# A fused convolution, linear-attention and mixture-of-experts block on one core: two small products and the reciprocals' low halves move from VectorE to GpSimd, and the program orders of the engines are written anew

## What is computed

```python
x = x + conv3x3(sign(batchnorm(groupnorm(x))), sign(W) * scale)      # L0
t = x as 3136 tokens of 32 channels
u = layernorm(t)
q, k, v = elu(u Wq)+1, elu(u Wk)+1, u Wv                               # 16 heads of 32
o = (q cos) (k cos)^T v + (q sin) (k sin)^T v;   denom = 1 / (q . sum(k) + 1e-5)
t = t + (o * denom) Wd + bd                                            # L1, linear attention
p = softmax(layernorm(t) Wr + br); the two largest of 8, scaled to sum 1
t = t + sum over those two of p_e * (layernorm(t) We + be)             # L2, two experts of 8
```

## Time and profile before

| | us |
|---|---|
| median of 3 runs | 2692.53 (2686.22 to 2696.71) |
| profiled execution, span from its first to its last instruction | 2691.5 |
| busy: PE / DVE / POOL / ACT | 2363.6 / 2278.2 / 1865.1 / 1743.1 |
| share of the span | 88% / 85% / 69% / 65% |

### The profile page before, as it was taken

How to read it: one execution, slowest core, us unless ns; L and a number is a source line. 1 busy time by engine, 2 the same in 40 slices (tenths; PEclk the granted TensorE clock), 3 DMA queues, 4 the chain that set the end, 5 groups by cost and what they waited for, 6 DMA issues and landing times.

```text
span 2691.5 us, 57490 instructions
## 1 busy us (share of the span) xinstructions
PE 2363.6 (88%) x19300; PEld 1162.4 (43%) x19300; DVE 2278.2 (85%) x2849; ACT 1743.1 (65%) x2821; POOL 1865.1 (69%) x1479
## 2 busy tenths in 40 slices
PE   3479999999999999998999999899898999999972
PEld 3324444444444444444444444444444444444442
DVE  4457999898998989898898989999898989999973
ACT  0167777676776767666776767777676767777630
POOL 0124777777777777776777777777777777777677
PEclk7589999999999999999999999999999999999995
DMA  9200000000000000000000000000000000000000
GB/s 261 34 13 10 11 16 17 10 8 17 17 17 17 17 17 5 14 17 17 17 16 17 6 12 17 17 17 16 18 12 7 16 17 17 17 11 7 7 7 12
DMA packets 235817, 55.16 MB, mean 20 GB/s; under 512 B 229648, under 2 KB 230528, under 8 KB 235360
## 3 DMA queue, kind: packets, MB, share of 16 engines
q1 hardware_dynamic: 235488, 50.96, 9.4%
HBM read 31.19 MB, written 12.85 MB: 16 GB/s over the span
## 4 chain that ended last, share of the span: by engine, by line
PE 41%; DVE 32%; issue 17%; ACT 5%; POOL 2%; DMA 1%; DVEq 1%; SPq 1%; ACTq 0%; POOLq 0%
PE ps L606 7%; DVE kbuf L987 7%; PE ps L581 6%; DVE qbuf L993 5%; PE ps L572 4%; PE ps L623 4%; PE ps L597 3%; PE ps L564 3%; DVE route L1052 3%; PE ps L657 3%; PE ps L632 3%; DVE prod L1077 2%; DVE rs L1010 2%; ACT ebuf L717 2%; PE ps L645 2%
## 5 line engine op out<-in xcount | busy, mean ns | idle before, releaser
L712 ACT ACTIVATE ebuf<-ps,small 112x1024 f32<-112x1024 f32 x448 | 498.5, 1113 | 279.0 <-PE ps L572 242.0
L987 DVE SCALAR_TENSOR_TENSOR kbuf<-ps,ebuf 112x1024 f32<-112x1024 f32 x448 | 542.7, 1211 | 113.1 <-ACT ebuf L712 110.1
L811 POOL TENSOR_TENSOR qbuf<-spread_r,qbuf 128x896 f32<-128x896 f32 x224 | 473.9, 2116 | 179.4 <-ACT spread_r L747 179.3
L993 DVE SCALAR_TENSOR_TENSOR qbuf<-ps,ebuf 128x896 f32<-128x896 f32 x448 | 485.8, 1084 | 84.5 <-ACT ebuf L717 62.6
L717 ACT ACTIVATE ebuf<-ps,small 128x896 f32<-128x896 f32 x448 | 451.4, 1008 | 122.8 <-PE ps L597 71.1
L581 PE MATMUL ps<-kbuf,xcs 112*64 112x512 f32 x1792 | 488.8, 624 | 39.1 <-issue 32.7
L789 POOL TENSOR_TENSOR rstd<-varr,power 112x28 f32<-112x28 f32 x64 | 307.2, 4800 | 183.1 <-DVE varr L977 179.5
L632 PE MATMUL ps<-qbuf,gmat 128*64 128x224 f32 x3584 | 387.5, 358 | 39.4 <-DVE pbuf L1021 35.9
L840 POOL TENSOR_TENSOR prod<-prod 112x512 f32<-112x512 f32 x224 | 285.7, 1276 | 103.0 <-DVE prod L1077 103.0
L747 ACT ACTIVATE spread_r<-ps 128x896 f32<-128x896 f32 x224 | 205.5, 917 | 171.1 <-PE ps L623 162.0
L632 PEld LDWEIGHTS ps<-qbuf,gmat 128*64 128x64 f32 x3584 | 237.0, 137 | 157.0 <-DVE pbuf L1021 44.0
(11 more groups left out here) (133 smaller groups left out, 3530.2 us busy)
## 6 DMA issues: line engine op xcount, KB each, us to landing
qbuf<-in_x SPq DMA_DIRECT2D x8, 1568.0 KB, 11.6
xt<-in_x SPq DMA_DIRECT2D x256, 49.0 KB
out<-ffn SPq DMA_DIRECT2D x256, 49.0 KB
shifted<-nat SPq DMA_DIRECT2D x128, 52.6 KB, 5.0
qbuf<-in_sel SPq DMA_DIRECT2D x1, 1024.0 KB, 11.8
tabn<-in_tabnc SPq DMA_DIRECT2D x1, 784.0 KB, 13.5
p<-in_p2c SPq DMA_DIRECT2D x1, 528.0 KB, 10.4
tabd<-in_tabdc SPq DMA_DIRECT2D x1, 448.0 KB, 11.0
```

What stands on the lines that cost most here:

```text
L712: act.activation(ebuf[0:PT, 0, :].rearrange("p (a b) -> p a b", a=2), o[0:PT, :, :], ACT.Exp, bias=minus_one[0:PT, :]).then_inc(kexp_made, 1)
L811: nc.gpsimd.tensor_tensor(qbuf[:, 2:4, n, :], spread_r[:, :, :], qbuf[:, 2:4, n, :], ALU.mult)\
L987: v.scalar_tensor_tensor(kbuf[:, n % 2, :].rearrange("p (a b) -> p a b", a=2), o[0:PT, :, :], 1.0, ebuf[0:PT, 0, :].rearrange("p (a b) -> ...
L993: v.scalar_tensor_tensor(qbuf[:, k0:k0 + 2, j, :], o[:, :, 0:G * PT], 1.0, ebuf[:, 1, 0:2 * G * PT].rearrange("p (a b) -> p a b", a=2), AL ...
```

## The change

Four things are changed.

1. The remainder (RL) is made by POOL, one instruction for each half. It reads `den` and `r_high` in all 128 partitions, spread twice over the columns, and writes all of `rs`; ACT then overwrites one quadrant pair for each half of the columns with the high part (a new step RH, two copies that read `r_high`, behind a wait for POOL).
2. The two products of marks and rank (RF) are made by POOL. DVE's next reduction waits for each.
3. The first reduction and the first marking of the routing read the logits out of PSUM; DVE's copy is gone, and ACT makes it (LG on ACT), behind a wait for both DVE readers. The PSUM slot is given back by ACT's copy.
4. `schedule` and `SHIFTS` are replaced by one table of places for each engine (`ORDER`).

```diff
-SCHEDULE = schedule()
+ORDER = {
+    "tensor": {
+        "RP": [12.95, 13.20, 14.05, 15.50, 17.85, 18.99, 20.75],
...
+    "gpsimd": {
+        "RL": [13.11, 17.30],
+        "RF": [32.19, 33.81],
...
-                "LG": (route_step, 16), "F": (prod_made, 7), "XC": (xc_made[0], 1), "ZT": (z_made[0], 2), "ZU": (z_made[1], 2),
+                "LG": (logits_kept, 1), "F": (prod_made, 7), "XC": (xc_made[0], 1), "ZT": (z_made[0], 2), "ZU": (z_made[1], 2),
```

On ACT:

```diff
                 elif kind == "RC":
...
                     act.activation(r_high[:, :], den[:, 0:HALFW], ACT.Copy).then_inc(rhigh_made, 1)
+                elif kind == "RH":
+                    act.wait_ge(r_made, m.at(2, n + 1))
                     for c in range(2):
-                        last = act.activation(rs[0:64, n, HALFW * c:HALFW * (c + 1)], den[64 * c:64 * c + 64, 0:HALFW],
-                                              ACT.Copy)
+                        last = act.activation(rs[64 - 64 * c:128 - 64 * c, n, HALFW * c:HALFW * (c + 1)],
+                                              r_high[64 * c:64 * c + 64, :], ACT.Copy)
                     last.then_inc(r_rows_made, 1)
...
+                elif kind == "LG":
+                    act.wait_ge(route_step, m.at(13, 2))
+                    act.activation(route[:, 0, :], o[0:PT, 0, 0:SLOTS * EXPERTS], ACT.Copy).then_inc(logits_kept, 1)
```

On POOL:

```diff
+                elif kind == "RL":
+                    pool.wait_ge(rhigh_made, m.at(2, n + 1))
+                    both = [128, 2, HALFW]
+                    nc.gpsimd.tensor_tensor(rs[:, n, :].rearrange("p (c t) -> p c t", c=2),
+                                            den[:, 0:HALFW].unsqueeze(1).to_broadcast(both),
+                                            r_high[:, :].unsqueeze(1).to_broadcast(both), ALU.subtract).then_inc(r_made, 1)
+                elif kind == "RF":
+                    pool.wait_ge(route_step, m.at(13, 2 if n == 0 else 7))
+                    hot = route[:, 1 + n, :]
+                    nc.gpsimd.tensor_tensor(hot, hot, first[:, :], ALU.mult).then_inc(hot_ranked, 1)
```

On DVE:

```diff
-                elif kind == "RL":
-                    dve.wait_ge(rhigh_made, m.at(2, n + 1))
...
-                    last.then_inc(r_made, 1)
...
-                elif kind == "LG":
-                    dve.wait_ge(ring_full, no + 1)
-                    v.tensor_copy(route[:, 0, :], o[0:PT, 0, 0:SLOTS * EXPERTS]).then_inc(route_step, 1)
...
+                    if kind == "LG":
+                        src = grid(o[0:PT, 0, 0:SLOTS * EXPERTS])
+                        dve.wait_ge(ring_full, no + 1)
+                        v.tensor_reduce(top1, src, AX_X, ALU.max).then_inc(route_step, 1)
+                        after(1)
+                        v.tensor_tensor(grid(hot1), src, spread(top1), ALU.is_equal).then_inc(route_step, 1)
+                    elif n in (0, 3):
+                        hot, w = (hot1, w1) if n == 0 else (hot2, w2)
+                        dve.wait_ge(hot_ranked, m.at(2, 1 if n == 0 else 2))
                         v.tensor_reduce(w, grid(hot), AX_X, ALU.max).then_inc(route_step, 1)
```

More of the change, by code:

```diff
@@ L134 @@
 MISC = ("XT", "CV", "DN", "SU", "NM", "T2")
[L137 to L178, removed]
-SCHEDULE = schedule()
-SHIFTS = {
-    "tensor": {},
[8 rows of a table removed]
+ORDER = {
+    "tensor": {
[17 rows of a table added]
+    },
+    "vector": {
[14 rows of a table added]
+    },
+    "scalar": {
[19 rows of a table added]
+    },
+    "gpsimd": {
+        "CS": [-4.50, 0.07],
+        "F": [36.34, 37.08, 38.65, 38.98, 39.96, 42.60, 45.49],
+        "T2": [20.05, 22.69, 27.21, 29.06],
+        "RP": [15.17, 16.29, 17.14, 17.41, 17.78, 19.92, 22.27],
+        "PN2": [30.96],
+        "PL2": [31.25],
+        "RL": [13.11, 17.30],
+        "PN1": [-10.28],
+        "RF": [32.19, 33.81],
+        "OUT": [47.31],
+        "PL1": [-7.26],
+        "GT": [36.20],
+    },
+    "sync": {
+        "CV": [-27.47],
+        "XT": [-34.18],
+        "OUT": [37.44],
+    },
 }
@@ L198, in iteration @@
 def iteration(engine, i):
-    shift = SHIFTS[engine]
-    steps = sorted((t + shift.get(kind, 0), t, kind, n) for t, kind, n in SCHEDULE)
     out = []
-    for t, t0, kind, n in steps:
-        d = int(t // PERIOD)
-        out.append((t - PERIOD * d, t0, kind, i - d, n))
-    return [(kind, m, n) for _, _, kind, m, n in sorted(out) if 0 <= m < B]
+    for kind, times in ORDER[engine].items():
+        for n, t in enumerate(times):
+            d = int(t // PERIOD)
+            out.append((t - PERIOD * d, kind, i - d, n))
+    return [(kind, m, n) for _, kind, m, n in sorted(out) if 0 <= m < B]
 ITERATIONS = range(-3, B + 3)
@@ L411, in build @@
         route_step = sem("route_step")
+        logits_kept = sem("logits_kept")
+        hot_ranked = sem("hot_ranked")
         ratio_made = sem("ratio_made")
@@ new lines, in step @@
+                        v.tensor_reduce(top1, src, AX_X, ALU.max).then_inc(route_step, 1)
[4 more added lines that the diff above has]
+                        dve.wait_ge(hot_ranked, m.at(2, 1 if n == 0 else 2))
+                        v.tensor_reduce(w, grid(hot), AX_X, ALU.max).then_inc(route_step, 1)
+                    elif n == 1:
+                        after(3)
+                        v.tensor_tensor(grid(hot1), grid(hot1), spread(w1), ALU.is_equal).then_inc(route_step, 1)
+                        dve.wait_ge(logits_kept, m.at(1, 1))
+                        after(4)
+                        v.scalar_tensor_tensor(rest, hot1, -3.0e38, logits, ALU.mult, ALU.add).then_inc(route_step, 1)
@@ L1068, in step @@
                         v.reciprocal(w2, w1).then_inc(route_step, 1)
-                        after(15)
+                        after(12)
                         v.tensor_tensor(w1, ratio, w2, ALU.mult).then_inc(route_step, 1)
```

38 lines of the change are left out of this document (11 added, 27 removed), and 57 rows, old and new, of tables (ORDER, SHIFTS).

## The result

The changed kernel takes 2704.44 us, the median of 5 runs (2701.85 to 2710.61). The kernel before takes 2690.14 us (5 runs, 2686.22 to 2696.71). The ratio is 1.0061, with a 95% interval of 1.0042 to 1.0081: 0.6% slower, where 3.1% faster was forecast. 2704 lies outside the range of 2550 to 2690.

The account below looks back on a forecast made before the run. PE and DVE were taken to bound the kernel in turn, with 4.5 us of winnable idle PE per image; 3.1 us of it over 27 images gives 84 us, 2691.5 to 2608 us, 3.1% faster; range 2550 to 2690.

Parts of the forecast that it names:

- the slack of 4.1 us: Ahead of PE's first spreading: 9.2 us of other work against a 5.1 us path through remainder and copies, left for queueing.
- Slower: Rival, chance 0.13: the remainder is stuck in POOL's queue behind F steps, PE waits 5.8 us an image; 2765 us.
- 1.2 us per image that this change doesn't touch, since the loop keeps its form: PE's holes of about 2.7 us, one in each loop pass, 32.7 us in all, taken as unchanged.
- most of the 4.5 goes: PE's idle time per image: if DVE-held stretches become like the PE-held one, most goes; 3.1 us taken.
- freed 6.66 us: DVE's time per image removed: four remainders 3.90, two rank products 2.38, the logits' copy 0.38, at mean durations.
- The 0.89 us before the first spreading: PE's wait for DVE's remainder before its first spreading, counted as winnable idle time per image.
- the cap: PE's winnable idle time, 4.5 us per image: routing 1.54, reciprocals 1.65, before the first spreading 0.89, elsewhere 0.4.
- 34 us as the alternative: Gain by the engine-selection rule: at DVE's shortest durations only 2.7 us per image are freed, giving 2658 us.
- my 84: Whole forecast gain in us: 3.1 us per image, some 70% of PE's winnable idle time, over 27 images.
- The lower end is 0: PE's order might leave the same holes: Lower bound of the gain per image from PE's idle time, whose upper bound was 4.5 us.
- The stall moves instead of going: Rival, chance 0.14: DVE's remaining markings stall beside POOL, 2.45 us per image comes back, leaving 0.65; 2675 us.
- PE's busy time per image rises: Sign that the sum is wrong at its limit of 4.5 us of idle PE per image.

Follow-up runs that it names:

- p1_flat: The changed instructions on the program orders of before, with images 3 to 28 written out instead of looped: 2588.30 us, 0.963 of the kernel before.
- e6_mark: The changed kernel with DVE's last marking L1069 placed two steps later, behind NM3 and K13, loop as before: 2687.19 us, 0.9973 of the kernel before.
- p1_new_work_old_order: The changed instructions on the program orders of before, loop as before: 2634.08 us, 0.9786 of the kernel before.

## Why the prediction was wrong

The medians give the change as a sum. Written out, 2618.8 becomes 2588.3 by the moved work: **-30.5**. The new table adds the late marking: 2625.8 instead of 2588.3 written out, **+37.5**. The loop costs 78.6 us instead of 71.8: **+6.8**. Together +13.8, which is 2704.4 less 2690.6. On the old table it would have been -30.5 and, by a loop that costs 45.8 instead of 71.8, -26.0: -56.5.

*What held.* DVE's lines are gone, and DVE has 64.3 us per image (forecast 62.8); the first marking out of PSUM takes 0.39 us, no more than before. On the new table PE's first spreading no longer waits, so the slack of 4.1 us sufficed there and the rival "Slower", a remainder stuck in POOL's queue, did not happen. POOL's new lines were a little dearer than their nearest rows (0.95 and 0.57 forecast), over 26 or 27 images:

```profile
L827 POOL TENSOR_TENSOR rs<-den,r_high 128x448 f16<-128x448 f32 x53 | 55.0, 1039 | 70.2 <-ACT r_high L738 70.2
L833 POOL TENSOR_TENSOR route<-route,first 112x224 f32<-112x224 f32 x54 | 35.8, 663 | 43.3 <-DVE route L1066 43.3
```

*The first step that failed* is "1.2 us per image that this change doesn't touch, since the loop keeps its form". I priced a pass by PE's hole in the earlier trace rows, 2.7 us. Written out, the kernel before is 71.8 us faster, 5.5 us a pass, 2.8 us per image. PE still idles 3.9 us per image there, so 3.9 and not 4.5 could be won by moving work; the rest of the loop's price lies in PE's busy time, 71.9 us per image in the loop and 71.0 without it. And the price is not left alone by a new table, even with the same loop: 6.0 us a pass as changed, 7.6 with the marking mended (2687.2 against 2588.1), 3.5 on the old table, 6.0 when that table is only cut at other steps.

*The second* is "most of the 4.5 goes", 3.1 us per image. Written out the moved work gives 30.5 / 27 = 1.1 us: PE idles 3.2 us per image in p1_flat where it idled 3.9. My estimate took DVE's freed 6.66 us and a share of PE's idle time, and asked of no single hole what ends it next. The 0.89 us before the first spreading, which the cap counts as won, show it: on the old orders they are a wait of 1.2 us for ACT. The rule of "GPSIMD Engine Reference", section "4.1 Engine selection", in the Trainium skill, by which I worked out 34 us as the alternative, came nearer to the 30.5 written out; in the loop, 56 us on the old table lie between it and my 84. That is luck in part: DVE lost 3.7 us of busy time per image written out, 69.0 less 65.2, and not the 2.7 of that sum.

*The third* is the bound: "The lower end is 0: PE's order might leave the same holes". A new order can bring holes of its own, and this one did. The rival "The stall moves instead of going" named the mechanism: the remaining markings have means of 1.26 and 1.57 us over 27 images,

```profile
L1069 DVE TENSOR_TENSOR route<-route,rmax 112x224 f32<-112x224 f32 x27 | 42.4, 1571 | 0.9
L1058 DVE TENSOR_TENSOR route<-route,rmax 112x224 f32<-112x224 f32 x27 | 34.1, 1262 | 0.9
```

but I priced it as DVE's lost time, against a gain, and put it at 2675. Its price is PE's: a hole of 2.1 us in 21 of 27 images, and matmuls at 1.2 GHz behind 17 of these. Written out it is 37.5 us, 1.4 per image, less than the rival's 2.45; but it met a gain of 1.1 and not of 3.1. The order of the change was there to be read: L1028 stands behind the last marking. "PE's busy time per image rises" was among the signs of a wrong cap, and it rose from 71.9 to 73.4.

*Still open.* Of the 7.6 us a pass that the boundary of the new table costs with the marking mended, PE's two holes are 4.7 (34.2 and 21.6 us over 12 boundaries in e6_mark). As an estimate from that trace, some 3 us are the low clock: it is 0.94 to 0.96 over the images with a boundary, of 81.8 us on average. The old table cut at the same steps pays 6.0, and there 5.0 us are holes and the clock is 1.00 in 11 of 12 of these images. Why the clock falls more often on the new table is not shown. That DVE, no longer close to the end, makes the loop cheaper on the old table (3.5 against 5.5) is argued from its busy time and not shown; the low clock, at 11 of 12 boundaries before and at 5 of 12 in p1_new_work_old_order, can be a part of it.

## What to carry to other kernels

A table of orders is a change of its own: run the moved work on the old table and the old work on the new one before either is judged, and write the loop out once to see what its passes cost. A stall is priced by what stands behind it on its engine and who waits for that, so it may be enough to move one step. Where a pass is cut matters like any other place in the order: best where the holes of the engines lie over each other, so that none of them waits for another's.
